# Cross attention on one Trainium2 core: query stacks in 6 transfers for 12, key parts written one by one, the sums read back later in the queue's order

## The chip, the cores and the metric

The kernel runs on one core of a Trainium2 chip. The metric is the device time of one execution in microseconds (us), the median of the timed runs. Five engines work side by side: TensorE (PE in the profile, with PEld for its weight loads), VectorE (DVE), ScalarE (ACT), GpSimd (POOL) and SyncE (SP). SP computes nothing here; it issues nearly all transfers between device memory (DRAM) and on-chip memory (SBUF), one after another, in the order in which they are written, and waits on semaphores between them.

## The reference

Four layers in a row on `x` of shape (32, 100, 128), with a context `ctx` of (32, 1444, 128) and a condition of (32, 128). Layers 0, 1 and 3 are transformer layers: modulated layer norm, self attention, cross attention to the context, feed forward. Layer 2 is a router with three experts. The change lies in the cross attention of the three transformer layers (here layer 3's; 16 heads of 8 channels, 100 queries, 1444 keys, 32 batches):

```python
xn = _ln(x)
q = _heads(xn @ q_w + q_b)
kv = (context @ kv_w + kv_b).reshape(B, S, 2, H, HD)
k = kv[:, :, 0].transpose(0, 2, 1, 3)
v = kv[:, :, 1].transpose(0, 2, 1, 3)
x_ca = _attend(q, k, v) @ ca_proj_w + ca_proj_b     # softmax(q k^T * SCALE) v, float32
x = x + x_ca
```

## The kernel before

All is float32, but scores go through bf16 matmuls: a float32 query or key is split into three bf16 parts (high, middle, low), and six of the nine products of parts are added up inside one matmul, whose contracted rows hold 8 channels times 6 slots (48 rows, `CROWS`), for the 8 heads of one half `e` of the array at rows 64·e and up. `SLOT_Q` and `SLOT_K` say which part stands in which slot. So each batch needs a query stack `qst` (48 rows for each half, 8 heads × 100 tokens along a row) and a key stack `kst` (128 rows × 8 heads × 1444 keys) in SBUF. Both come from DRAM: the query parts lie in `g.qx` from an earlier phase, and the key stack is put together in DRAM (`g.kscr`), because one key part goes to several slots.

`cross_attention_phase` is called for layers 0, 1 and 3 with `context` "normed", "raw" and "kept"; these words name the three phases below. It works as a pipeline over 32 batches, one slot for each batch; three buffers (`LAG`) of every kind turn. In slot b:

- PE makes the transposed context, keys and values of batches b+3 and b+2 (`pe_prep`), score tiles of batches b+1 and b+2 for the row maxima only (`pe_max`, line 1169, 48 tiles a batch, read by DVE at line 1349), then the transposed scores of batch b (`pe_scores`, line 1192), of which ACT takes exponentials (line 1296), and their products with the values (`pe_values`, line 1209). The order on PE is written out in `PLANS`.
- DVE turns the maxima of b+1 into three bf16 parts `nparts` (`dve_negmax`, the last step is line 1373). `pe_scores` of the next slot starts only when these lie in the query stack (`neg_loaded`).
- POOL splits the keys of b+3 into `parts` (`pool_split_keys`: for each cut of the columns copy, subtract, copy, subtract, lines 1401, 1428, 1401, 1432). One cut in the normed phase, three in the others. Before it overwrites `parts` it waits until the former batch's key transfers have landed (`k_written`).
- SP runs `sp_slot`, the queue order at issue here: `sp_stacks` (b+2; it waits for `k_written`, then loads `kst`, one transfer at line 1460, and `qst`, twelve at line 1467), `sp_load_ctx` (b+5), `sp_out` (b-1: the sums `osb` go to DRAM, line 1496; SP waits until they have landed; four transfers bring them back into `oT`, line 1500, and one the denominators into `den`), in the raw phase `sp_keep_ctx` (line 1481), `sp_negmax` (b+1, six at line 1476), `sp_keys_out` (b+3, six at line 1489).

The lines of that order are

```python
if slot.k(2) is not None:
    sp_stacks(slot.k(2))
if slot.k(5) is not None:
    sp_load_ctx(slot.k(5))
if slot.k(-1) is not None:
    sp_out(slot.k(-1))
...
if slot.k(1) is not None:
    sp_negmax(slot.k(1))
if slot.k(3) is not None:
    sp_keys_out(slot.k(3))
```

PE needs the stacks of b+2 about two thirds into slot b (tile 0 of `pe_max`), and the negative maxima of b+1 at the start of slot b+1.

Of the kernel before, what the change touches and what calls it, by code (L numbers as in the profile page):

```python
# [11 lines left out]
B = 32  # L12
N = 100
S = 1444
T = B * N
HEADS = 16
HD = P // HEADS
# [4 lines left out]
PAIRS = HEADS // 2  # L22
# [13 lines left out]


PARTS = 3
SLOT_K = (0, 1, 2, 0, 1, 0)
SLOT_Q = (0, 0, 0, 1, 1, 2)  # L40
HALF = 64
CROWS = HD * len(SLOT_K)
CROWS_NEG = CROWS + 3
# [7 lines left out]
def wait(eng, sem, value):  # L51

    if isinstance(value, int) and value <= 0:
        return
    eng.wait_ge(sem, value)
# [965 lines left out]
def cross_attention_phase(g, wk, kb, wv, context):  # L1021
# [15 lines left out]
    S1 = 6 if kept else 9  # L1037
    CUTS = [(0, S)] if normed else [(0, BANK), (BANK, 2 * BANK), (2 * BANK, S)]
    ST_BANK, O_BANK, RING = 0, 4 * BANK, 5 * BANK
    K_RUNS = ((0, 3), (3, 2), (5, 1))  # L1040
    KW = 16 * 2 * len(K_RUNS)
    Q_SLOTS = ((0, 3), (3, 2), (5, 1))

    plan = PLANS[context]
    PREP_INDEX = ({"K0": 0, "K1": 1, "K2": 2, "V0": 3, "V1": 4, "V2": 5} if kept else
# [7 lines left out]
    with ExitStack() as st:  # L1053
# [15 lines left out]
        parts = sb("kparts", [P, 3, S], BF16)  # L1069
# [9 lines left out]
        split, parts_ready = sem("split_steps"), sem("parts_ready")  # L1079
        k_written, k_loaded = slots("k_written"), slots("k_loaded")  # L1080
        qst_loaded, neg_loaded = slots("qstack_loaded"), slots("negmax_loaded")
# [9 lines left out]
        def slot_rows(s, e, first, n):  # L1091

            return g.kscr[s].rearrange("(e r d) (j n) -> e (d j) r n", e=2, d=HD, j=PAIRS)[e, :, first:first + n]

        def max_tile(slot, x):

            return (slot.k(1), x + MAX_A) if x < MT - MAX_A else (slot.k(2), x - (MT - MAX_A))
# [5 lines left out]
        def pe_ring_free(slot, tile):  # L1103

            for t, back in older[tile]:
                if t == "turn":
                    k = slot.k(1 + back)
                    if k is not None:
                        wait(g.pe, neg_steps, 4 * (k.b + 1))
                        return  # L1110
                elif isinstance(t, str):
                    k = slot.k((2 if t[0] == "V" else 3) + back)
                    if k is not None:
                        wait(g.pe, p_read, S1 * k.b + PREP_INDEX[t] + 1)
                        return
                else:
                    k = slot.k((1 if t < MT - MAX_A else 2) + back)
                    if k is not None:
                        wait(g.pe, m_read, MT * k.b + (t + MAX_A) % MT + 1)
                        return  # L1120
# [35 lines left out]
        def pe_max(slot, x):  # L1156

            k, t = max_tile(slot, x)
            if k is None:
                return  # L1160
            s, r = k.s, k.r
            if t == 0:
                wait(g.pe, k_loaded[s], 16 * (r + 1))
                wait(g.pe, qst_loaded[s], 16 * 12 * (r + 1))
            pe_ring_free(slot, x)
            at = bank_of(x)
            e, c, j = t % 2, (t // 2) % 3, t // 6
            a, w, row0 = starts[c], widths[c], HALF * e
            nc.tensor.matmul(ps[0:N, at:at + w], g.qst[s][row0:row0 + CROWS, j, :], g.kst[s][row0:row0 + CROWS, j, a:a + w],  # L1169
                             start=True, stop=True).then_inc(m_full, 1)  # L1170
# [246 lines left out]
        def pool_split_keys(k):  # L1417
# [3 lines left out]
            p = k.prev()  # L1421
            wait(pool, k_written[p.s], KW * (p.r + 1))
            for i, (a, z) in enumerate(CUTS):
# [18 lines left out]
        def sp_load_ctx(k):  # L1442
            b, s, r = k.b, k.s, k.r
            sp = g.sp
            if kept:
                wait(sp, p_full, S1 * (b - LAG + 1))
                sp.dma_start(turned[s][:, :], g.ctxT[b]).then_inc(ctx_loaded[s], 16)
                return
            wait(sp, p_full, S1 * (b - LAG) + 3)
            full = KT - 1  # L1450
            sp.dma_start(ctok[s][:, 0:full, :], g.ctx[bass.ds(b, 1), 0:128 * full, :].rearrange("a (k p) c -> p (a k) c", p=P)).then_inc(ctx_loaded[s], 16)
            sp.dma_start(ctok[s][0:kts[-1], full, :], g.ctx[bass.ds(b, 1), 128 * full:S, :].rearrange("a p c -> p (a c)")).then_inc(ctx_loaded[s], 16)

        def sp_stacks(k):

            b, s, r = k.b, k.s, k.r
            sp = g.sp
            wait(sp, st_full, H2 * (b - LAG + 1))
            wait(sp, k_written[s], KW * (r + 1))
            sp.dma_start(g.kst[s][:, :, :].rearrange("p j n -> p (j n)"), g.kscr[s]).then_inc(k_loaded[s], 16)  # L1460
            per = CH // N
            for e in range(2):
                for part, (first, copies) in enumerate(Q_SLOTS):
                    src = g.qx[b // per, e, part].rearrange("(d j) n -> d j n", j=PAIRS)[:, :, N * (b % per):N * (b % per) + N]
                    for slot in range(first, first + copies):
                        at = HALF * e + HD * slot
                        sp.dma_start(g.qst[s][at:at + HD, :, :], src).then_inc(qst_loaded[s], 16)

        def sp_negmax(k):
            b, s, r = k.b, k.s, k.r  # L1470
# [7 lines left out]
        def sp_keep_ctx(k):  # L1478
            b, s, sp = k.b, k.s, g.sp
            wait(sp, p_read, S1 * b + PREP_INDEX["T2"] + 1)  # L1480
            sp.dma_start(g.ctxT[b], turned[s][:, :]).then_inc(ctx_kept, 16)

        def sp_keys_out(k):
            b, s, r = k.b, k.s, k.r
            sp = g.sp
            wait(sp, parts_ready, len(CUTS) * (b + 1))
            for first, n in K_RUNS:
                for e in range(2):
                    sp.dma_start(slot_rows(s, e, first, n), parts[HALF * e:HALF * e + HALF, 0:n, :]).then_inc(k_written[s], 16)

        def sp_out(k):

            b, s, r = k.b, k.s, k.r
            sp = g.sp
            wait(sp, o_read, b + 1)
            sp.dma_start(g.oscr[s], osb[s][:, :]).then_inc(o_moved[s], 16)
            wait(sp, o_moved[s], 96 * r + 16)
            src = g.oscr[s].rearrange("(c r) (a n) -> a c r n", r=32, n=N)
            for a in range(4):
                sp.dma_start(g.oT[32 * a:32 * a + 32, bass.ds(b * N, N)], src[a, :, 0:HD, :]).then_inc(o_moved[s], 16)  # L1500
            per = CH // N
            sp.dma_start(g.den[b // per:P:NCH, N * (b % per):N * (b % per) + N], src[:, :, HD, :]).then_inc(o_moved[s], 16)

        def sp_slot(slot):
            if slot.k(2) is not None:
                sp_stacks(slot.k(2))
            if slot.k(5) is not None:
                sp_load_ctx(slot.k(5))
            if slot.k(-1) is not None:
                sp_out(slot.k(-1))  # L1510
            if context == "raw" and slot.k(3) is not None:
                sp_keep_ctx(slot.k(3))
            if slot.k(1) is not None:
# [3 lines that stand above are left out]
# [3 lines left out]
        known = lambda b: Slot(0, b, LAG, False)  # L1520
        looped = lambda i, u: Slot(i, u, LAG, True)
        first = known(0).k(0)

        with nc.Block() as block:
# [69 lines left out]
            @block.sync  # L1594
            def _(sp):
                g.sp = sp
                for b in range(LAG - 1):
                    sp_load_ctx(known(b).k(0))
                if normed:
                    sp.wait_ge(stacks_set, 1)  # L1600
                    for s in range(LAG):
                        for e in range(2):
                            rows = slice(HALF * e + CROWS, HALF * e + HALF)
                            sp.dma_start(g.kscr[s][rows, :], g.kst[0][rows, :, :].rearrange("p j n -> p (j n)")).then_inc(ones_written, 16)
                    sp.wait_ge(ones_written, 16 * 2 * LAG)
                for b in range(-3, 1):
                    sp_slot(known(b))
                for i in range(loops):
                    for u in range(1, LAG + 1):
                        sp_slot(looped(i, u))  # L1610
                for b in range(LAG * loops + 1, B):
                    sp_slot(known(b))
                sp_out(known(B - 1).k(0))
                if context == "raw":
                    sp.wait_ge(ctx_kept, 16 * B)
                for s in range(LAG):
                    sp.wait_ge(o_moved[s], 96 * len(range(s, B, LAG)))
# [573 lines left out]
```

## Time and profile before

| | |
|---|---|
| median of 3 runs | 5570.83 us (5566.85 to 5578.4) |
| the profiled execution | 5582.41 us, span of its instructions 5580.6 us |
| mean granted clock of TensorE | 0.864 of full speed |
| cross attention "normed" (layer 0) | from about 425 to 1712 us |
| cross attention "raw" (layer 1) | from about 2140 to 3354 us |
| cross attention "kept" (layer 3) | from about 4310 to 5472 us |
| busy share of the span | PE 86%, DVE 70%, ACT 53%, POOL 26% |

The table is read so: the profiled execution is one run of its own, 11.6 us above the median of the timed ones; a change in us that is worked out from its rows is subtracted from the median. The shares are means over phases with different limits, so they say little on a single phase; the three cross attentions together take some 3660 us, two thirds of the span, and what limits each is read from its own stretch.

### The profile page before, as it was taken

The numbers are of one execution on the slowest core, as the hardware profiler recorded it, in microseconds if no ns is written. First come the engines' busy times: TensorE is split into PE (matmuls) and PEld (weight loads), VectorE is DVE, ScalarE is ACT, GpSimd is POOL, SyncE is SP. The second block draws the span as 40 slices with busy tenths as digits, with TensorE's granted clock in tenths as the row PEclk, the third lists the DMA queues.
The fourth block names the chain that finished last, engine by engine and source line by source line (L and its number), as shares of the span: only waits on it lengthen the run. The fifth ranks groups of instructions, "written<-read, shape, count | busy, mean of one in ns | idle before, by whom it ended". The sixth has DMA issues, their size and how long they took to land. (4 is left out here: it accounts for less than half of the span.)

```text
span 5580.6 us, 168125 instructions
## 1 busy us (share of the span) xinstructions
PE 4790.3 (86%) x72434; PEld 3025.4 (54%) x72434; DVE 3913.3 (70%) x7814; ACT 2961.3 (53%) x4527; POOL 1466.4 (26%) x1189
## 2 busy tenths in 40 slices
PE   4858999999998585999999997888676799999998
PEld 2634555555554362666666663564364366656654
DVE  5547888888883553888888873465454688889893
ACT  2323666766655332666666663215423366666665
POOL 1013444434420103333333310000200334333320
PEclk6667999999988666999999988999766699999998
DMA  3325555555530334666666630550242565556640
GB/s 81 69 62 174 158 166 172 156 180 159 165 125 10 77 61 140 198 205 206 204 200 201 193 118 18 166 175 1 53 71 54 173 188 188 185 186 193 190 155 17
DMA packets 481664, 766.00 MB, mean 137 GB/s; under 512 B 144922, under 2 KB 381882, under 8 KB 468538
## 3 DMA queue, kind: packets, MB, share of 16 engines
q1 hardware_dynamic: 462394, 741.14, 44.5%
q10 hardware_dynamic: 18528, 14.11, 1.1%
q8 instruction: 571, 9.36, 0.7%
q14 instruction: 171, 1.40, 0.1%
HBM read 465.48 MB, written 287.75 MB: 135 GB/s over the span
## 5 line engine op out<-in xcount | busy, mean ns | idle before, releaser
L1349 DVE TENSOR_REDUCE maxima<-ps 100x1 f32<-100x482 f32 (+1 forms) x4608 | 2743.0, 650 | 580.3 <-PE ps L1169 566.5
L1296 ACT ACTIVATE probs<-ps 128x800 f32<-128x800 f32 (+1 forms) x2304 | 1805.6, 833 | 573.6 <-PE ps L1192 562.7
L1169 PE MATMUL ps<-kst,qst 48*100 48x482 bf16 (+1 forms) x4608 | 1392.6, 420 | 137.1 <-DMA qst<-cross_q_parts 54.9
L1401 POOL TENSOR_TENSOR kparts<-kf,zero 128x512 bf16<-128x512 f32 (+2 forms) x448 | 545.0, 1217 | 2044.2 <-ACT kf L1268 2004.1
L1209 PE MATMUL ps<-probs,vals 128*9 128x100 f32 x36864 | 1047.9, 256 | 1.0 <-ACT probs L1296 0.9
L1209 PEld LDWEIGHTS ps<-probs,vals 128*9 128x9 f32 x36864 | 757.5, 92 | 240.3 <-issue 198.8
L1169 PEld LDWEIGHTS ps<-kst,qst 48*100 48x100 bf16 x4608 | 443.8, 123 | 797.7 <-DVE maxima L1349 452.5
L1192 PE MATMUL ps<-qst,kst 51*128 51x100 bf16 x18432 | 803.8, 210 | 81.2 <-ACT probs L1296 60.6
L1192 PEld LDWEIGHTS ps<-qst,kst 51*128 51x128 bf16 x18432 | 614.4, 99 | 224.9 <-issue 86.4
L763 ACT ACTIVATE probs<-ps 100x800 f32<-100x800 f32 x192 | 159.7, 837 | 369.0 <-PE ps L711 368.6
L1146 PE MATMUL ps<-ctxT,perm_wk_L 128*128 128x512 f32 (+1 forms) x576 | 327.6, 656 | 31.9 <-DMA ctxT<-ctx_turned 17.1
L1268 ACT ACTIVATE kf<-ps,perm_b_L 128x512 f32<-128x512 f32 (+1 forms) x288 | 190.4, 662 | 271.9 <-PE ps L1146 255.8
L1274 ACT ACTIVATE vals<-ps 128x512 f32<-128x512 f32 (+1 forms) x288 | 162.1, 563 | 317.2 <-PE ps L1152 312.0
L1432 POOL TENSOR_TENSOR kparts<-kf,kparts 128x512 bf16<-128x512 f32 (+2 forms) x224 | 305.0, 1361 | 17.6
L1428 POOL TENSOR_TENSOR kf<-kf,kparts 128x512 f32<-128x512 f32 (+2 forms) x224 | 304.7, 1360 | 17.6
L775 DVE TENSOR_REDUCE maxima<-ps 100x4 f32<-100x400 f32 x384 | 205.6, 570 | 143.6 <-PE ps L689 142.8
L1152 PE MATMUL ps<-wkv_L,ctxT 128*128 128x128 f32 (+1 forms) x1536 | 262.7, 318 | 7.2 <-DVE maxima L1349 4.9
L689 PE MATMUL ps<-kst 96*100 96x100 bf16 x1152 | 142.7, 286 | 131.7 <-DMA kst<-k_parts 103.3
L1152 PEld LDWEIGHTS ps<-wkv_L,ctxT 128*128 128x128 f32 (+1 forms) x1536 | 211.1, 211 | 66.8 <-DVE maxima L1349 44.6
L1262 ACT ACTIVATE ctxT<-ps 128x512 f32<-128x512 f32 (+1 forms) x192 | 109.8, 572 | 178.8 <-PE ps L1138 178.8
L689 PEld LDWEIGHTS ps<-kst 96*100 96x100 bf16 x1152 | 118.0, 191 | 157.1 <-issue 105.1
L1138 PE MATMUL ps<-ident,ctok 128*128 128x128 f32 (+1 forms) x768 | 135.8, 295 | 63.7 <-POOL ctok L1414 43.4
(260 smaller groups left out, 4528.0 us busy)
## 6 DMA issues: line engine op xcount, KB each, us to landing
kst<-ctx_k_stack SPq DMA_DIRECT2D x96, 2888.0 KB
ctx_k_stack<-kparts SPq DMA_DIRECT2D x192, 541.5 KB
ctx_k_stack<-kparts SPq DMA_DIRECT2D x192, 361.0 KB
ctok<-in_ctx_dram SPq DMA_DIRECT2D x64, 704.0 KB
ctx_k_stack<-kparts SPq DMA_DIRECT2D x192, 180.5 KB
ctx_turned<-ctxT SPq DMA_DIRECT2D x32, 722.0 KB, 3.4
cT<-ctx_turned SPq DMA_DIRECT2D x32, 722.0 KB, 5.5
ctxT<-ctx_turned SPq DMA_DIRECT2D x32, 722.0 KB
```

What stands on the lines that cost most here:

```text
L689: ins = nc.tensor.matmul(ps[0:N, o:o + N], queries[s][0:SROWS, h // 2, q0:q0 + N], keys[0:SROWS, h // 2, k0:k0 + N], start=True, stop=True)
L775: nc.vector.tensor_reduce(maxima[:, t // 4, c:c + 4], ps[0:N, at:at + CH].rearrange("p (h k) -> p h k", h=4), AX.X, ALU.max).then_inc(m_re ...
L1146: ins = nc.tensor.matmul(ps[:, at:at + w], wk, turned[s][:, a:a + w], start=True, stop=True)
L1152: ins = nc.tensor.matmul(ps[0:n, at + 128 * q:at + 128 * q + 128], turned[s][:, 128 * kt:128 * kt + n], wv, start=True, stop=True)
L1169: nc.tensor.matmul(ps[0:N, at:at + w], g.qst[s][row0:row0 + CROWS, j, :], g.kst[s][row0:row0 + CROWS, j, a:a + w], start=True, stop=True). ...
L1192: ins = nc.tensor.matmul(ps[0:kts[kt], o:o + N], g.kst[s][rows, 4 * hf + jj, 128 * kt:128 * kt + kts[kt]], g.qst[s][rows, 4 * hf + jj, :], ...
L1209: ins = nc.tensor.matmul(ps[q:q + VW, o:o + N], vals[s][:, kt, h, :], probs[kt % 2][hf][:, N * (4 * e + jj):N * (4 * e + jj) + N], start=( ...
L1296: nc.scalar.activation(probs[kt % 2][hf][0:kts[kt], :].rearrange("p (k n) -> p k n", k=2), src, ACT.Exp).then_inc(exp_done, 1)
L1349: nc.vector.reduce_max(maxima[:, col:col + 1], ps[0:N, at:at + widths[c]], AX.X).then_inc(m_read, 1)
L1401: return nc.gpsimd.tensor_tensor(out, src, g.zero[0:src.shape[0], 0:1].to_broadcast(list(src.shape)), ALU.add)
L1428: nc.gpsimd.tensor_tensor(kf[:, a:z], kf[:, a:z], parts[:, 0, a:z], ALU.subtract).then_inc(split, 1)
L1432: nc.gpsimd.tensor_tensor(parts[:, 2, a:z], kf[:, a:z], parts[:, 1, a:z], ALU.subtract).then_inc(parts_ready, 1)
```

## The change

Three edits in `cross_attention_phase`. (1) The two tables of slots change places, so that the query slots hold parts 0, 1, 2, then 0, 1, then 0; the same six products are added up in another order. A run of slots now holds consecutive query parts, which lie one after the other in DRAM, so one transfer fills a run: 3 for each half, 6 for 12, with 24, 16 and 8 rows. (2) A run of key slots now holds copies of one part: part 0 goes to three slots, part 1 to two, part 2 to one. The six key transfers keep their sizes and places in DRAM, read one part repeatedly (`to_broadcast`) and each pair waits for its own part only: part 0 and 1 for steps 1 and 3 of POOL's last cut. (3) `sp_out` is cut in two: the sums go out before `sp_load_ctx` is issued, and are read back (`sp_out_back`) after it.

```diff
-SLOT_K = (0, 1, 2, 0, 1, 0)
-SLOT_Q = (0, 0, 0, 1, 1, 2)
+SLOT_K = (0, 0, 0, 1, 1, 2)
+SLOT_Q = (0, 1, 2, 0, 1, 0)
...
             for e in range(2):
-                for part, (first, copies) in enumerate(Q_SLOTS):
-                    src = g.qx[b // per, e, part].rearrange("(d j) n -> d j n", j=PAIRS)[:, :, N * (b % per):N * (b % per) + N]
-                    for slot in range(first, first + copies):
-                        at = HALF * e + HD * slot
-                        sp.dma_start(g.qst[s][at:at + HD, :, :], src).then_inc(qst_loaded[s], 16)
+                rows = g.qx[b // per, e].rearrange("t (d j) n -> (t d) j n", j=PAIRS)
+                for first, n in RUNS:
+                    at = HALF * e + HD * first
+                    sp.dma_start(g.qst[s][at:at + HD * n, :, :],
+                                 rows[0:HD * n, :, N * (b % per):N * (b % per) + N]).then_inc(qst_loaded[s], 16)
...
         def sp_keys_out(k):
             b, s, r = k.b, k.s, k.r
             sp = g.sp
-            wait(sp, parts_ready, len(CUTS) * (b + 1))
-            for first, n in K_RUNS:
+            for part, (first, n) in enumerate(RUNS):
+                if part < 2:
+                    wait(sp, split, 3 * (len(CUTS) * (b + 1) - 1) + (1, 3)[part])
+                else:
+                    wait(sp, parts_ready, len(CUTS) * (b + 1))
                 for e in range(2):
-                    sp.dma_start(slot_rows(s, e, first, n), parts[HALF * e:HALF * e + HALF, 0:n, :]).then_inc(k_written[s], 16)
+                    sp.dma_start(slot_rows(s, e, first, n),
+                                 parts[HALF * e:HALF * e + HALF, part:part + 1, :].to_broadcast([HALF, n, S])).then_inc(k_written[s], 16)
...
             sp.dma_start(g.oscr[s], osb[s][:, :]).then_inc(o_moved[s], 16)
+
+        def sp_out_back(k):
...
             wait(sp, o_moved[s], 96 * r + 16)
...
+            if slot.k(-1) is not None:
+                sp_out(slot.k(-1))
             if slot.k(5) is not None:
                 sp_load_ctx(slot.k(5))
             if slot.k(-1) is not None:
-                sp_out(slot.k(-1))
+                sp_out_back(slot.k(-1))
```

On SP, in a slot of the kept phase, these rows stood from one key stack's load to the read back of the sums (`kst`, `qst` the stacks, `ctxT` the context, `o_sums` the sums in DRAM):

```order
L1460 DMA kst_417<-ctx_k_stack 128x11552
L1467 DMA qst_417<-cross_q_parts 8x8x100 x12
L1447 DMA ctxT_507<-ctx_turned 128x1444
L1496 DMA o_sums<-osb_507 128x400
L1500 DMA oT<-o_sums 32x1x100 x4
L1502 DMA den<-o_sums 16x1x100
L1476 DMA qst_417<-nparts 1x8x100 x6
```

The same place after the change:

```order
L1459 DMA kst_417<-ctx_k_stack 128x11552
L1465 DMA qst_417<-cross_q_parts 24x8x100
L1465 DMA qst_417<-cross_q_parts 16x8x100
L1465 DMA qst_417<-cross_q_parts 8x8x100
L1465 DMA qst_417<-cross_q_parts 24x8x100
L1465 DMA qst_417<-cross_q_parts 16x8x100
L1465 DMA qst_417<-cross_q_parts 8x8x100
L1499 DMA o_sums<-osb_507 128x400
L1446 DMA ctxT_507<-ctx_turned 128x1444
L1508 DMA oT<-o_sums 32x1x100 x4
L1510 DMA den<-o_sums 16x1x100
L1475 DMA qst_417<-nparts 1x8x100 x6
```

Six transfers stand where twelve stood, and the write of the sums has moved ahead of the context's load, its read back has stayed behind it.

The key transfers of the same slot, before, with their waits (`modulated_29` is the number that `parts_ready` has here):

```order
L1476 DMA qst_417<-nparts 1x8x100 x5
L1489 DMA ctx_k_stack<-kparts 64x3x1444 [waits modulated_29]
L1489 DMA ctx_k_stack<-kparts 64x3x1444
L1489 DMA ctx_k_stack<-kparts 64x2x1444 x2
L1489 DMA ctx_k_stack<-kparts 64x1444 x2
```

and after (`scaled_28` is the number of `split`, the count of POOL's steps):

```order
L1475 DMA qst_417<-nparts 1x8x100 x5
L1491 DMA ctx_k_stack<-kparts 64x3x1444 [waits scaled_28]
L1491 DMA ctx_k_stack<-kparts 64x3x1444
L1491 DMA ctx_k_stack<-kparts 64x2x1444 [waits scaled_28]
L1491 DMA ctx_k_stack<-kparts 64x2x1444
L1491 DMA ctx_k_stack<-kparts 64x1444 [waits modulated_29]
L1491 DMA ctx_k_stack<-kparts 64x1444
```

The six transfers have kept their shapes and their place in the queue; one wait became three, of which only the last is for the end of POOL's split.

## Rows read from the trace of the kernel before

**Rows 1.** One line's instructions, raw phase, steady stretch: the row maxima, one a batch.

```profile
L1355 DVE TENSOR_REDUCE rowmax<-maxima x29: 202/203/204, 2263.8 to 3252.9; 100x16 f32<-100x48 f32 x29
```

**Rows 2.** The same, kept phase, steady stretch.

```profile
L1355 DVE TENSOR_REDUCE rowmax<-maxima x29: 202/203/204, 4435.9 to 5381.1; 100x16 f32<-100x48 f32 x29
```

**Rows 3.** Windows: us, busy us (instructions) of each engine, granted clock, DMA share, GB/s.

```profile
2555.90:2589.90 34.00, 33.75 (x677) 21.57 (x670) 30.00 (x55) 24.15 (x35) 12.46 (x12) 1.00 0.64 204
...
2802.10:2841.10 39.00, 38.91 (x668) 25.30 (x670) 29.06 (x53) 24.10 (x34) 12.45 (x12) 0.84 0.62 192
4650.90:4682.90 32.00, 31.35 (x660) 20.25 (x656) 29.71 (x55) 22.30 (x32) 12.47 (x12) 1.00 0.62 197
```

**Rows 4.** Waits of PE, raw, 2308 to 3263 us: total us, times, longest.

```profile
PE ps L1192 <- DMA qst<-nparts: 17.2, 14, 2.5
```

**Rows 5.** Waits of PE, kept, 4478 to 5391 us.

```profile
PE ps L1169 <- DMA kst<-ctx_k_stack: 6.6, 4, 2.0
```

**Rows 6.** Waits of SP, raw, 2308 to 3263 us.

```profile
SPq L1476 <- DVE nparts L1373: 9.1, 5, 2.3
```

**Rows 7.** Waits of SP, kept, 4430 to 5390 us.

```profile
SPq L1500 <- DMA o_sums<-osb: 115.3, 28, 5.5
...
SPq L1476 <- DVE nparts L1373: 9.8, 2, 9.2
```

**Rows 8.** Waits of SP, normed, 530 to 1580 us.

```profile
SPq L1476 <- DVE nparts L1373: 76.6, 27, 6.8
SPq L1489 <- POOL kparts L1432: 53.2, 27, 2.0
```

**Rows 9.** Timeline of SP, one kept slot: start us, us, line, transfer.

```profile
4725.74 0.33 SPq L1460 DMA_DIRECT2D kst<-ctx_k_stack  x1
4726.11 8.34 SPq L1467 DMA_DIRECT2D qst<-cross_q_parts  x12
...
4734.98 0.43 SPq L1496 DMA_DIRECT2D o_sums<-osb  x1
4739.74 2.55 SPq L1500 DMA_DIRECT2D oT<-o_sums  x4
...
4747.45 9.29 SPq L1489 DMA_DIRECT2D ctx_k_stack<-kparts  x6
4759.26 0.33 SPq L1460 DMA_DIRECT2D kst<-ctx_k_stack  x1
```

**Rows 10.** Transfers from 4725 to 4745 us: GB/s in 40 slices of 0.5 us.

```profile
GB/s 6 0 0 647 92 0 462 277 554 323 554 370 370 554 277 601 310 462 79 110 116 268 174 277 393 396 349 130 13 33 0 0 26 18 12 21 58 13 3 0
...
ctxT<-ctx_turned SPq DMA_DIRECT2D x1, 722.0 KB
```

**Rows 11.** Timeline of SP, end of the kept phase: the last sums.

```profile
5471.34 0.32 SPq L1496 DMA_DIRECT2D o_sums<-osb  x1
5473.23 2.54 SPq L1500 DMA_DIRECT2D oT<-o_sums  x4
```

**Rows 12.** Single lines: ns of one issue on SP, min/median/max, first and last start.

```profile
L1467 SPq DMA_DIRECT2D qst<-cross_q_parts x1152: 632/646/1328, 426.3 to 5407.4; - x192
```

**Rows 13.** The same, the negative maxima.

```profile
L1476 SPq DMA_DIRECT2D qst<-nparts x576: 634/635/1588, 484.9 to 5448.5; - x192
```

**Rows 14.** The same, the context's load.

```profile
L1451 SPq DMA_DIRECT2D ctok<-in_ctx_dram x64: 384/448/1087, 381.1 to 3178.6; - x64
```

**Rows 15.** Timeline of PE, start of the raw phase: the first maximum tile.

```profile
2187.27 0.64 PE L1169 MATMUL ps<-kst,qst 48*100 48x482 bf16 x2 [25.62 <-DMA qst<-cross_q_parts]
```

**Rows 16.** Timeline of POOL, start of the raw phase: the last cut of the first split.

```profile
2160.59 0.89 POOL L1401 TENSOR_TENSOR kparts<-kf,zero 128x420 bf16<-128x420 f32 x1
...
2163.57 0.98 POOL L1432 TENSOR_TENSOR kparts<-kf,kparts 128x420 bf16<-128x420 f32 x1
```

**Rows 17.** Timeline of SP, start of the raw phase.

```profile
2164.57 8.59 SPq L1489 DMA_DIRECT2D ctx_k_stack<-kparts  x6
2175.38 0.36 SPq L1460 DMA_DIRECT2D kst<-ctx_k_stack  x1
```

More of the change, by code:

```diff
@@ L1039, in cross_attention_phase @@
     ST_BANK, O_BANK, RING = 0, 4 * BANK, 5 * BANK
-    K_RUNS = ((0, 3), (3, 2), (5, 1))
-    KW = 16 * 2 * len(K_RUNS)
-    Q_SLOTS = ((0, 3), (3, 2), (5, 1))
+    RUNS = ((0, 3), (3, 2), (5, 1))
+    KW = 16 * 2 * len(RUNS)
     plan = PLANS[context]
@@ L1163, in pe_max @@
                 wait(g.pe, k_loaded[s], 16 * (r + 1))
-                wait(g.pe, qst_loaded[s], 16 * 12 * (r + 1))
+                wait(g.pe, qst_loaded[s], 16 * 2 * len(RUNS) * (r + 1))
             pe_ring_free(slot, x)
@@ L1496, in sp_out @@
             sp.dma_start(g.oscr[s], osb[s][:, :]).then_inc(o_moved[s], 16)
+        def sp_out_back(k):
+            b, s, r = k.b, k.s, k.r
+            sp = g.sp
             wait(sp, o_moved[s], 96 * r + 16)
@@ L1613, in _ @@
                 sp_out(known(B - 1).k(0))
+                sp_out_back(known(B - 1).k(0))
                 if context == "raw":
```

## The prediction, made before the changed kernel had run

> **What bounds the kernel now.** I read the stage windows first and took the three cross attentions apart, because two thirds of the span lie there and the diff touches nothing else. Then I took for each phase the time per batch, SP's waits, PE's waits, and single slots.
>
> Time per batch is read from an instruction that runs once a batch. In the raw phase 28 intervals take 3252.9 − 2263.8 = 989.1 us, 35.33 us each [rows 1]; in the kept phase 5381.1 − 4435.9 = 945.2 us, 33.76 each [rows 2].
>
> Is that PE's pace? Three slots answer, each cut from the first score matmul to the next one [rows 3]. One raw slot takes 34.0 us with PE busy for 33.75 of them, one kept slot 32.0 with 31.35. These are what PE's own work takes when nothing holds it: the floors. A third slot with the same work takes 39.0 us, at a mean granted clock of 0.84 for 1.00, so part of it ran at 1.2 for 2.4 GHz. It begins at 2802.1, right after a wait of PE for the negative maxima; PE had such waits in 14 of the raw slots [rows 4], and in the kept phase waits for the key stack [rows 5]. So short waits for transfers, and the low clock after them, make up the 1.3 and 1.8 us between mean and floor.
>
> Why are the transfers late? SP's waits tell. In the normed phase SP waits for DVE's maxima in each of 27 slots, 76.6 us, and for POOL, 53.2 us [rows 8]: it is early by 4.8 us a slot, and engines set the pace. In the raw phase the first of these waits has shrunk to 9.1 us in 27 slots [rows 6], in the kept phase to 9.8 in 28, nearly all of it in one [rows 7]. There SP goes round without waiting for any engine; what it still waits for is transfers of its own, such as 115.3 us in 28 slots for the sums to land, 4.1 us a slot [rows 7]. One kept turn shows it [rows 9]: from 4725.74 to 4759.26, 33.52 us, issues and landings end to end. **In raw and kept the queue on SP sets the pace**, by 1.3 and 1.8 us a slot over PE.
>
> **The change part by part.**
>
> *Sums ahead of the context's load.* In that turn the sums are issued at 4734.98 and have landed by 4739.74, after 4.76 us; the last ones of the phase, with an empty queue, land in 1.89 us (5471.34 to 5473.23) [rows 11]. What stands before them is read from the slices [rows 10]: the key stack runs from about 4726.5 to 4734, a slow stretch with the query rows to about 4736.5, then 722 KB of context and the sums at some 390 GB/s until 4739. So transfers are served about in the order of issue, and the sums, 200 KB, came last. Without the context ahead of them they land 722 × 1024 B / 390 GB/s = 1.9 us earlier, say 2.0 with the 0.44 us issue. That is the lower bound. The upper adds half of the slow stretch of 2.5 us, if six query transfers need half the time of twelve: 3.3 us. I take the middle, 2.6.
>
> *Six query transfers for twelve.* Issue of one takes 0.646 us [rows 12], so up to 6 × 0.65 = 3.9 us less. But this doesn't add to the 2.6: the sums behind still wait for the key stack ahead of them, which runs to about 8.3 us after its issue. Issued earlier, they only wait longer. The saving is covered by that stack; if the cover were gone it would be 3.9. The price of a 24-row transfer is in no row. Eight short runs cost 0.635 us [rows 13], 64 cost 0.646 [rows 12], a load of 1408 runs (11 × 128 in its shape) 0.448 [rows 14]: no growth with the count, so I take 0.65; the other end is three times that, 1.94 for 24 rows, and no saving at all.
>
> The Trainium skill speaks against this edit: in Perfetto Trace Analysis, section What "DMA-bound" means, the issuing engine's track is time of descriptor generation, and large descriptors are what helps. Here the runs stay 200 B and their number stays the same, so by that rule the twelve times 0.65 us would remain. The three rows above disagree with it as far as they go; what it gives is the second case below.
>
> *Key parts one by one.* In the steady slots the sizes and the order stay, and SP arrives after POOL has finished in raw and kept, so nothing is gained but room. In the normed phase the start moves up 2 us a slot, which is slack. It counts at the start of a phase: in the raw one POOL's first step of the last cut ends at 2161.48, the last at 2164.55 [rows 16], and the keys go at 2164.57 [rows 17]. The first pair can go 3.1 us earlier. The first maximum tile follows the key stack's issue by 11.9 us (2175.38 [rows 17] to 2187.27 [rows 15]), waiting for the query rows; with half as many I take 1 us off (0 to 1.8). PE had been idle for 25.62 us, so all 4 us come off the phase. The other two starts have the same steps; 3 × 4 = 12 us.
>
> *The new turn of the queue.* Kept: 33.76 − 2.6 = 31.2 us (30.5 to 31.8), raw at least the same off: 35.33 − 2.6 = 32.7. Both are under the floors of 32.0 and 34.0, by 0.8 and 1.3 us, so SP begins to wait for DVE's maxima as in the normed phase, PE no longer waits, and the low clock after its waits goes. What is late next is PE itself. In kept the margin is small, so I put 32.2 for 32.0. Gains: raw (35.33 − 34.0) × 28 = 37 us, kept (33.76 − 32.2) × 28 = 44 us. The first and last three slots of a phase I leave as they are. Normed: no steady gain.
>
> **Sum:** 37 + 44 + 12 = 93 us. The profiled execution took 5582.41 us (span 5580.6 and 1.8 around it), which gives 5489; it lies 11.6 above the median of the timed runs, 5570.83, from which I forecast **5478 us**, 1.7% less. A difference under 0.2% (11 us) could not be told from none.
>
> **The rivals.**
>
> *The queue still sets the pace* (the query issues keep their time, or the sums gain only the 2.0). Then the turns are 31.8 and 33.3 before any unevenness, at the floors, and some slots still end in a wait and a low clock. For it: the spread of issue times, 632 to 1328 ns for one transfer [rows 12]; against: it needs both edits to do their least. Half the gain, 22 + 19, and 9 at the starts: 50 us, 5521.
>
> *The floors are not floors.* The short slots may be short because the wait before them let DVE, ACT and POOL run ahead, and then PE would be held by them. For it: single slots can't show what a long row of them takes. Against: DVE is busy for 30.0 of 34.0 us and 29.7 of 32.0, ACT for 24.2 and 22.3 [rows 3]. Then only the starts remain: 5559, a change at the edge of what can be told.
>
> *Slower: the repeated source.* Each key transfer now reads one SBUF row two or three times. From issue to landing the keys take 4747.45 to 4759.26, 11.8 us [rows 9]. If copies of one row are drawn one behind the other, this phase grows; from 2.6 us of growth (22%) the turn is as long as before, and beyond it the kernel is slower. At half as long again, +5.9 us: kept 31.2 + 5.9 = 37.1, raw 38.6, against 33.76 and 35.33, so (3.3 + 3.3) × 28 = 185 less the 12 of the starts: 5744. Against it: before, the three parts of a row came from the same partitions too, and the shapes of the transfers have not changed. The Trainium skill has a harder form of it: DMA: Bandwidth & Descriptors, Rules for kernel authors, says that a leading broadcast of c copies confines a transfer to at most c of the 16 engines. In the order's rows the leading count is still 64, not the copies, so the rule should not bite, and no run here shows such a case; that keeps this rival at its small chance.
>
> **How the numbers follow.** 0.62 for the forecast (its own range 5460 to 5500: floors met in full and the runs' spread of 6 us below, a kept slot of 32.8 above), 0.25 for the queue that still sets the pace, 0.08 for the false floors, 0.04 for slower, 0.01 for a gain beyond the floors. The range of 8 in 10 takes the forecast and most of the second case: 5450 to 5530. Faster by over 0.2%: 0.62 + 0.25 + 0.01 + a little of the third, 0.89; within: 0.07; slower: 0.04.
>
> **What would show it.** Time per batch of 34.0 and 32.2 us in raw and kept, no other in normed; SP waiting for DVE's maxima in nearly every slot of raw and kept; PE's waits for the maxima and the key stack gone, granted clock near 1.00 in the steady stretches; sums landed some 11.4 us after the key stack's issue (14.0 before); query issues of 0.65 us each whatever their rows; six key transfers in about 9 us as before; first maximum tiles 4 us earlier. Wrong if SP is early and time per batch stays (false floors), if query issues take 1.3 to 1.9 us, or if the keys take over 14 us from issue to landing.

## The result and the profile after

The changed kernel takes 5491.75 us (median of 4 runs, 5476.65 to 5503.66), the kernel before on the same chip 5574.61: a ratio of 0.9849 with a 95% interval of 0.9818 to 0.9879, 83 us less (67 to 101). Timed again beside other kernels (below) the ratio was 0.9838 (0.9816 to 0.9860), 90 us less. The profiled execution took 5503.66 us, span 5501.9.

Time per batch first: the row maxima in the steady stretch of raw, then of kept, as in [rows 1, 2].

```profile
L1354 DVE TENSOR_REDUCE rowmax<-maxima x29: 202/203/204, 2263.0 to 3214.6; 100x16 f32<-100x48 f32 x29
...
L1354 DVE TENSOR_REDUCE rowmax<-maxima x29: 202/203/203, 4394.5 to 5297.6; 100x16 f32<-100x48 f32 x29
```

Raw: 951.6 / 28 = 33.99 us for 35.33. Kept: 903.1 / 28 = 32.25 for 33.76. That is 37.5 + 42.1 = 80 us. The windows from a phase's first score matmul to its last batch's show what PE did in them (columns as in [rows 3]). First the kernel before, raw and kept:

```profile
2237.00:3263.00 1026.00, 1002.05 (x19316) 638.63 (x19313) 868.58 (x1567) 699.08 (x986) 361.08 (x348) 0.97 0.64 201
4411.00:5391.00 980.00, 930.94 (x18966) 599.45 (x18964) 864.51 (x1566) 646.67 (x899) 362.39 (x348) 0.97 0.60 189
```

and the changed one:

```profile
2237.00:3226.00 989.00, 979.53 (x19339) 625.38 (x19341) 866.57 (x1567) 699.90 (x988) 361.68 (x348) 1.00 0.67 209
4370.00:5308.00 938.00, 911.95 (x18973) 589.91 (x18968) 862.01 (x1567) 646.39 (x900) 362.72 (x348) 0.99 0.63 197
```

Same work, but PE is busy 22.5 and 19 us less for it, at a granted clock of 1.00 and 0.99 for 0.97, and idle less (9.5 for 24 us in raw, 26 for 49 in kept). DVE, ACT and POOL have not changed.

SP's waits in raw, then kept, then normed (530 to 1580 us), to be laid beside [rows 6 to 8]:

```profile
SPq L1475 <- DVE nparts L1372: 66.1, 29, 10.3
SPq L1508 <- DMA o_sums<-osb: 54.2, 28, 5.3
...
SPq L1508 <- DMA o_sums<-osb: 144.7, 28, 5.8
...
SPq L1475 <- DVE nparts L1372: 34.9, 19, 13.4
...
SPq L1475 <- DVE nparts L1372: 207.6, 27, 9.8
```

In raw SP now waits for DVE's maxima in every slot, in kept in 19: the queue has become early. Leaving out one wait of 10.3 and 13.4 us at a phase's start, it is 2.0 us a slot in raw and 0.8 in kept. PE's waits in raw no longer name a transfer; in kept three small ones are left (first raw, then kept):

```profile
PE ps L1168 <- DVE maxima L1348: 4.5, 28, 0.2
PE ps L1208 <- issue: 2.1, 5, 0.7
...
PE ps L1168 <- DMA kst<-ctx_k_stack: 3.5, 3, 1.4
PE ps L1168 <- issue: 3.0, 4, 1.4
```

Before, kept had more such waits than the four of [rows 5]. Thirteen more at the same line (4478 to 5391 us) have no releaser that the profile shows:

```profile
PE ps L1169 <- issue: 20.7, 13, 3.0
```

Those over 0.5 us end 12.0 to 13.4 us after a key stack's issue, where the first tile of a phase comes too (11.9 us), so they are taken here as waits for the stacks; of 17 with 27.3 us in all, 7 with 6.5 are left.

One kept turn of SP (once round its list, for one slot), beside the turn of [rows 9]:

```profile
4671.86 0.34 SPq L1459 DMA_DIRECT2D kst<-ctx_k_stack  x1
4672.24 4.85 SPq L1465 DMA_DIRECT2D qst<-cross_q_parts  x6
4677.14 1.71 SPq L1499 DMA_DIRECT2D o_sums<-osb  x1
4678.89 0.43 SPq L1446 DMA_DIRECT2D ctxT<-ctx_turned  x1
4684.38 2.55 SPq L1508 DMA_DIRECT2D oT<-o_sums  x4
...
4688.68 4.13 SPq L1475 DMA_DIRECT2D qst<-nparts  x6
4692.85 8.88 SPq L1491 DMA_DIRECT2D ctx_k_stack<-kparts  x6
4703.95 0.33 SPq L1459 DMA_DIRECT2D kst<-ctx_k_stack  x1
```

The query issues take 4.85 us for 8.34. The sums go out 5.3 us after the key stack for 9.2, but are read back 12.5 us after it for 14.0: of the 3.9 us won at the issue, 1.5 are left at the landing here. As a mean of 23 slots the read back comes 12.2 us after the key stack's issue in raw (15.2 before) and 12.3 in kept (14.5 before).

The start of the raw phase (SP, POOL's last step of the first split, the first maximum tile on PE):

```profile
2163.77 8.59 SPq L1491 DMA_DIRECT2D ctx_k_stack<-kparts  x6
2174.59 0.36 SPq L1459 DMA_DIRECT2D kst<-ctx_k_stack  x1
...
2165.84 0.98 POOL L1431 TENSOR_TENSOR kparts<-kf,kparts 128x420 bf16<-128x420 f32 x1
...
2186.25 0.64 PE L1168 MATMUL ps<-kst,qst 48*100 48x482 bf16 x2 [22.03 <-DMA qst<-cross_q_parts]
```

Against POOL's end (2166.82) the keys go 3.05 us earlier, and the first tile follows after 19.4 us for 22.7 in [rows 15, 16]: 3.3 us. The same difference is 3.0 us in normed and 4.2 in kept.

### The profile page after: what moved, and what is told of

Same layout as the page of the kernel before. It is cut to its first block and busy times, and to the rows that moved or that the text cites. A ratio compares the mean times of both kernels' runs of the same rounds, so it can differ in the third digit from the quotient of the medians.

```text
span 5501.9 us, 167549 instructions
## 1 busy us (share of the span) xinstructions
PE 4762.0 (87%) x72434; PEld 3010.4 (55%) x72434; DVE 3909.5 (71%) x7814; ACT 2963.6 (54%) x4527; POOL 1467.9 (27%) x1189
```

## The experiments

The question is which edit brought the 83 us, and through what. **Theory:** in raw and kept a slot takes PE's own time or SP's turn, whichever is longer; the sums, no longer waiting behind the context, brought the turn below PE's time. **Rival:** the 4 us of query issue that a slot saves are what counts. The ratios are to the kernel before, timed on the same chip.

**Each edit alone.** *Edit 3 alone*, twelve query transfers and one wait for the keys kept:

```diff
...
+            if slot.k(-1) is not None:
+                sp_out(slot.k(-1))
             if slot.k(5) is not None:
                 sp_load_ctx(slot.k(5))
             if slot.k(-1) is not None:
-                sp_out(slot.k(-1))
+                sp_out_back(slot.k(-1))
```

What moves is the sums' write; their read back keeps its place in the queue's order, behind the context's load.

> The kernel before with edit 3 alone: the sums' write goes ahead of the context's load; twelve query transfers, keys after one wait. Theory (the order of the sums does it): the sums are read back 12.3 to 12.6 us after the key stack's issue for 15 before, raw and kept fall to 34.0 to 34.2 and 32.3 to 32.6 us a batch, 65 to 75 us less than the kernel before. Rival (the query issues, 4 us a slot, do it): about a quarter to a half of the 83 us, 20 to 40 us less, with time per batch near 34.7 and 33.1.

0.9851 (0.9839 to 0.9864), 83 us less: as much as the whole change, and more than the 65 to 75 us expected. The sums are read back 12.8 (raw) and 12.5 us (kept) after the key stack's issue, 2.4 and 2.0 earlier than before (means of 23 slots). Per batch 33.87 and 32.30:

```profile
L1355 DVE TENSOR_REDUCE rowmax<-maxima x29: 202/203/204, 2264.9 to 3213.2; 100x16 f32<-100x48 f32 x29
...
L1355 DVE TENSOR_REDUCE rowmax<-maxima x29: 202/203/204, 4388.1 to 5292.4; 100x16 f32<-100x48 f32 x29
```

*Edit 1 alone* (six query transfers, the sums behind the context as before; as the two tables change places, the key transfers read one part repeatedly here too, after one wait for all):

```diff
...
-                wait(g.pe, qst_loaded[s], 16 * 12 * (r + 1))
+                wait(g.pe, qst_loaded[s], 16 * 2 * len(RUNS) * (r + 1))
...
+                rows = g.qx[b // per, e].rearrange("t (d j) n -> (t d) j n", j=PAIRS)
+                for first, n in RUNS:
...
```

> The kernel before with edit 1 alone: six query transfers for twelve, in the old order of the queue, keys after one wait for all. Theory: the 4 us of issue are freed, but the sums still wait behind key stack and context, and are read back 14.0 to 14.8 us after the key stack's issue (15 before); 0 to 25 us less. Rival (the query issues do it): read back near 12.5 us, 45 to 75 us less.

0.9968 (0.9956 to 0.9980), 18 us less. Where the rest of the saved issue time went stands, for kept, in SP's waits (4403 to 5379 us), beside the row for the sums in [rows 7]:

```profile
SPq L1500 <- DMA o_sums<-osb: 197.7, 28, 8.0
```

SP waits for the sums 82 us longer than before, 2.9 us a slot. The queries' issue takes 4.4 us a slot for 8.0 (means of 23 slots): of the 3.6 us saved, 2.9 became waiting for the same landing, and another 1.0 went into a longer issue of the context's load (1.47 us for 0.49).

In raw the saving went another way. SP waits for the sums as long as before (110.2 us in 27 slots from 2308 to 3263 us, 110.7 before), but the issue of the context's second load has grown (2237 to 3263 us; first the kernel before):

```profile
L1452 SPq DMA_DIRECT2D ctok<-in_ctx_dram x27: 496/810/2010, 2254.9 to 3179.1; - x27
...
L1451 SPq DMA_DIRECT2D ctok<-in_ctx_dram x27: 3170/4117/5400, 2255.4 to 3171.9; - x27
```

The queries take 4.47 us a slot for 7.98, the context's two loads 5.42 for 1.46 (means of 23 slots): nothing is freed ahead of the sums.

*Edit 2 alone* (keys part by part, with the tables changed and one part read repeatedly; twelve query transfers, old order):

```diff
...
-            wait(sp, parts_ready, len(CUTS) * (b + 1))
-            for first, n in K_RUNS:
+            for part, (first, n) in enumerate(RUNS):
+                if part < 2:
+                    wait(sp, split, 3 * (len(CUTS) * (b + 1) - 1) + (1, 3)[part])
+                else:
+                    wait(sp, parts_ready, len(CUTS) * (b + 1))
...
```

> The kernel before with edit 2 alone: key parts written one by one as they are made, from a source row read two or three times; twelve query transfers, old order of the queue. Theory: only the three starts of a phase are shorter, by some 3 us each, 9 us less in all (5 to 12), time per batch as before. Rival (waiting for the split paces the steady slots too): 20 us less or more. If the repeated source cost anything, keys from issue to landing over 12.5 us and a kernel that is slower.

0.9981 (0.9970 to 0.9992), 11 us less; per batch 35.23 and 33.63, the first tiles of normed, raw and kept 2.1, 3.1 and 3.7 us earlier against POOL's end. It is the starts, as the theory has it, and no cost of the repeated source shows: at the start of raw it is 10.9 us from the first key transfer's issue to the key stack's, for 10.8 before.

*Edits 1 and 2, without 3* (against the changed kernel):

```diff
-            if slot.k(-1) is not None:
-                sp_out(slot.k(-1))
             if slot.k(5) is not None:
                 sp_load_ctx(slot.k(5))
             if slot.k(-1) is not None:
-                sp_out_back(slot.k(-1))
+                sp_out(slot.k(-1))
```

> The changed kernel without edit 3: six query transfers and key parts one by one, but the sums' write behind the context's load as before. Theory: 10 to 35 us less than the kernel before, raw and kept at 34.9 to 35.3 and 33.2 to 33.7 us a batch. Rival (the query issues do it): 55 to 83 us less, time per batch like the changed kernel's 33.99 and 32.25.

0.9953 (0.9940 to 0.9966), 26 us less, per batch 34.73 (a little under the 34.9 to 35.3 expected) and 33.38. The rival's 55 us or more are excluded.

**What is left for the others once the sums go first.** The changed kernel again, and edits 2 and 3 with twelve query transfers:

```diff
-                rows = g.qx[b // per, e].rearrange("t (d j) n -> (t d) j n", j=PAIRS)
-                for first, n in RUNS:
...
+                for slot, part in enumerate(SLOT_Q):
...
```

> The changed kernel itself, timed beside the next three, since edit 3 alone gave 81.5 us of the 84. If the other two edits add nothing once the sums go ahead: 80 to 85 us less than before. If they add what they gave in the old order (24 us): 105 us less, which the interval of the first comparison (0.9818 to 0.9879) just excludes.

> The changed kernel with twelve query transfers of 8 rows, so edits 2 and 3 alone. Theory (with the sums ahead, SP has room in every slot and issue time is free): the same time as the changed kernel within 5 us. Rival (4 us of issue a slot still count): 15 us or more above it.

0.9838 (0.9816 to 0.9860) and 0.9836 (0.9815 to 0.9858): with the sums ahead, six transfers for twelve are worth nothing that can be told.

**Is it PE's own time that ends the gain?** The read back of the sums is moved behind the keys:

```diff
-            if slot.k(-1) is not None:
-                sp_out_back(slot.k(-1))
             if context == "raw" and slot.k(3) is not None:
                 sp_keep_ctx(slot.k(3))
             if slot.k(1) is not None:
                 sp_negmax(slot.k(1))
             if slot.k(3) is not None:
                 sp_keys_out(slot.k(3))
+            if slot.k(-1) is not None:
+                sp_out_back(slot.k(-1))
```

> The changed kernel with the read back of the sums put behind the key transfers, into the time in which SP waits for the keys to land; the wait for the sums (5.8 us a slot in kept) goes. Theory (PE's own work is the floor, 32.0 and 33.85 to 34.0): kept goes from 32.25 to 32.0, raw stays at 33.9, 3 to 10 us less than the changed kernel and no more. Rival (SP's turn is still what is felt): 28 x 2 us or more in raw and kept, over 50 us less.

0.9833 (0.9810 to 0.9857), not to be told from the changed kernel. Kept, a waits row of SP (4400 to 5290 us) and of its batches:

```profile
SPq L1475 <- DVE nparts L1372: 237.8, 28, 9.1
```

```profile
L1354 DVE TENSOR_REDUCE rowmax<-maxima x29: 202/203/204, 4384.3 to 5281.3; 100x16 f32<-100x48 f32 x29
```

SP now has 8.5 us to spare in every slot, and a batch takes 897.0 / 28 = 32.04 us. That is the floor of [rows 3], and it is real: beyond it SP's time buys nothing. Raw, where SP has 6.6 us to spare, takes 34.04.

**Queries and sums ahead of the key stack:**

```diff
+            if slot.k(2) is not None and (slot.looped or slot.b != -2):
+                sp_queries(slot.k(2))
+            if slot.k(-1) is not None:
+                sp_out(slot.k(-1))
             if slot.k(2) is not None:
                 sp_stacks(slot.k(2))
-            if slot.k(-1) is not None:
-                sp_out(slot.k(-1))
...
+            if not slot.looped and slot.b == -3:
+                sp_queries(slot.k(3))
             if slot.k(3) is not None:
                 sp_keys_out(slot.k(3))
```

> The changed kernel with the query rows and the sums' write issued ahead of the key stack, before SP waits for the keys to land (at a phase's start ahead of the first key transfers), so that neither waits behind 2.9 MB. Theory: the first maximum tile of a phase follows the key stack's issue by 8.3 us, not 11.5, 9 us off the three starts, and kept at 32.0: 10 to 17 us less than the changed kernel. Rival (the tile waits for the key stack's landing, not for the query rows): no change at the starts, 0 to 7 us less. A risk: six issues of 0.8 us ahead of the key stack make it later by 2 us a slot.

0.9874 (0.9854 to 0.9894), 14 us above the changed kernel timed beside it, by the medians: the theory's number was wrong, the risk named came true. SP and PE in kept (4366 to 5320 us):

```profile
SPq L1480 <- DVE nparts L1372: 275.8, 29, 13.5
```

```profile
PE ps L1168 <- DMA kst<-ctx_k_stack: 17.1, 19, 2.1
```

SP has over 9 us to spare a slot, and yet PE waits for the key stack in 19 slots, and a batch takes 918.5 / 28 = 32.80 us:

```profile
L1354 DVE TENSOR_REDUCE rowmax<-maxima x29: 202/203/204, 4392.7 to 5311.2; 100x16 f32<-100x48 f32 x29
```

The timeline shows why:

```profile
4721.05 4.79 SPq L1480 DMA_DIRECT2D qst<-nparts  x6
4725.89 8.78 SPq L1496 DMA_DIRECT2D ctx_k_stack<-kparts  x6
4734.71 4.36 SPq L1463 DMA_DIRECT2D qst<-cross_q_parts  x6
...
4739.60 0.43 SPq L1471 DMA_DIRECT2D kst<-ctx_k_stack  x1
```

From the maxima, whose time DVE sets, to the key stack's issue it takes 18.6 us, for 15.3 in the changed kernel. So there is a second limit beside the turn: the chain from the maxima over the keys to the stack. At the starts of raw and kept the first tile came another 1.6 and 1.1 us earlier, not 3: the tile still follows the key stack's issue by 10.1 and 10.2 us, so the stack itself needs most of the 11.5 us. In normed it came 3.5 us later, since SP was still issuing queries when the keys were ready.

**Is it what stands ahead of the sums?** In the kept phase each context is loaded twice, the second time into a buffer that nobody reads; once in the kernel before, where it stands ahead of the sums, once in edit 3 alone, where it stands behind them. The same line in both (PE also waits for both loads of a batch):

```diff
...
                 sp.dma_start(turned[s][:, :], g.ctxT[b]).then_inc(ctx_loaded[s], 16)
+                sp.dma_start(spare[s][:, :], g.ctxT[b]).then_inc(ctx_loaded[s], 16)
```

> The kernel before, with the context of each batch loaded twice in the kept phase (a second load of 722 KB into a spare buffer right behind the first), so twice as much stands ahead of the sums in the queue. Theory (the sums wait for what was issued ahead of them, and SP's turn paces the phase): the sums are read back 1.9 us later, kept goes from 33.76 to 35.5 us a batch or more, 45 to 60 us more than the kernel before; raw and normed as they were. Rival (the sums' place in the queue is not what counts): under 15 us more.

> The same second load in the kernel with edit 3 alone, where the context stands behind the sums' write. Theory: the same bytes are moved but nothing waits behind them, kept stays at 32.0 to 32.4 us a batch, ratio to the kernel before 0.985 as without the load. Rival (the bytes themselves cost, by traffic beside the other transfers): kept grows by as much as it does with the load ahead of the sums.

Ahead: 1.0095 (1.0076 to 1.0114), 53 us more. Behind: 0.9847 (0.9824 to 0.9870), as without the load. The kept batches of the first, 1002.5 / 28 = 35.80 us, and a slot:

```profile
L1356 DVE TENSOR_REDUCE rowmax<-maxima x29: 202/203/204, 4442.4 to 5444.9; 100x16 f32<-100x48 f32 x29
```

```profile
4714.90 0.33 SPq L1462 DMA_DIRECT2D kst<-ctx_k_stack  x1
...
4725.23 0.43 SPq L1498 DMA_DIRECT2D o_sums<-osb  x1
4730.85 2.55 SPq L1502 DMA_DIRECT2D oT<-o_sums  x4
```

and of the second, 900.8 / 28 = 32.17:

```profile
L1356 DVE TENSOR_REDUCE rowmax<-maxima x29: 202/203/204, 4396.6 to 5297.4; 100x16 f32<-100x48 f32 x29
```

The sums are read back 16.0 us after the key stack (14.0 in [rows 9]; means 16.8 and 14.5), 2.0 us later here and 2.3 as a mean, and the batch grows by 2.0 us. The bytes themselves cost nothing that shows. This pair shows the theory best: 722 KB are worth 2 us a slot where something waits behind them, and nothing behind the sums.

**The context behind the read back**, and then behind the maxima too:

```diff
-            if slot.k(5) is not None:
-                sp_load_ctx(slot.k(5))
             if slot.k(-1) is not None:
                 sp_out(slot.k(-1))
+            if slot.k(5) is not None:
+                sp_load_ctx(slot.k(5))
```

> The kernel before with the context's load put behind the read back of the sums, so that the sums wait neither for it nor does it use their landing time. Theory: the sums are read back 12.5 us after the key stack's issue as with edit 3 alone, 60 to 85 us less than the kernel before. Rival (the gain of edit 3 is that the context is loaded while SP waits for the sums): under 25 us less.

0.9914 (0.9890 to 0.9938), 48 us less: between the two, so neither number came. The sums are read back 12.7 us after the key stack, as expected, and kept comes to 32.49 us; but raw stays at 982.5 / 28 = 35.09, with 13 waits of PE (2240 to 3260 us; 14 before, [rows 4]) for the maxima, which now stand behind the context:

```profile
L1355 DVE TENSOR_REDUCE rowmax<-maxima x29: 202/203/204, 2268.1 to 3250.6; 100x16 f32<-100x48 f32 x29
...
PE ps L1192 <- DMA qst<-nparts: 12.8, 13, 2.3
```

The second step, against the first:

```diff
+            if slot.k(1) is not None:
+                sp_negmax(slot.k(1))
             if slot.k(5) is not None:
                 sp_load_ctx(slot.k(5))
             if context == "raw" and slot.k(3) is not None:
                 sp_keep_ctx(slot.k(3))
-            if slot.k(1) is not None:
-                sp_negmax(slot.k(1))
```

> The kernel before with the context's load (and in raw the write of its turned copy) put behind the negative maxima as well, so that neither the sums nor the maxima stand behind it. It asks why raw stayed at 35.1 us a batch with the context right behind the sums. If the maxima's landing behind the context's bytes held PE there: raw comes to 34.0 to 34.3, PE's waits for the maxima go, some 75 us less than the kernel before. If it is SP's turn, which now holds the context's three issues (1.5 to 2 us) outside the sums' landing time: raw stays at 34.9 to 35.2, about 48 us less.

0.9942 (0.9919 to 0.9965), 32 us less, neither the 75 of the first case nor the 48 of the second. PE's waits for the maxima are gone, yet raw takes 973.5 / 28 = 34.77 us, just under the 34.9 to 35.2 of the second case, and kept 32.74. In PE's waits of raw (2290 to 3180 us) others stand in their place, ahead of the maximum tiles:

```profile
L1355 DVE TENSOR_REDUCE rowmax<-maxima x29: 202/203/204, 2259.2 to 3232.7; 100x16 f32<-100x48 f32 x29
...
PE ps L1169 <- issue: 15.0, 15, 2.6
```

The first tile of a batch follows the key stack's issue by 12.7 us (mean of 23 slots; 15.0 with edit 3 alone), close to the 12.0 at the phase's start where it waits for the stacks, and SP waits for DVE's maxima in only 2 of these slots. So raw is held by SP's turn, and the wait only moves from the maxima to the stacks. The turn carries the context's issues outside the sums' landing time, which the expectation named; what it did not name is that the six key issues, now right behind the context, take 9.8 us a slot for 8.6 with edit 3 alone. The order of edit 3 does both: the sums go early, and the context's issue lies in the time in which SP waits for them anyway.

## Why the prediction was right

| its term | predicted | measured |
|---|---|---|
| raw, per batch | 34.0, 37 us in all | 33.99, 37.5 us |
| kept, per batch | 32.2, 44 us | 32.25 and 32.05, 42 and 48 us |
| three starts | 12 us | 3.0 + 3.3 + 4.2 = 10.5 us |
| sums read back after the key stack's issue | 11.4 us | 12.2 and 12.3 |
| SP's turn, raw and kept | 32.7 and 31.2 | about 32.0 and 31.5 (batch less SP's wait for DVE) |
| in all | 93 us | 83 and 90 us |

*The queue paces raw and kept.* Right: in kept the doubled context brought the sums 2.3 us later and the batch grew by 2.0, and in raw edit 3 alone brought them 2.4 us earlier and the batch fell from 35.33 to 33.87. Normed had room and did not move (38.80 before, 38.92 and 38.83 after).

*The sums ahead of the context.* This was the step that carried the forecast, and alone it gave all of the steady gain. The size of 2.6 us was near: 2.2 in kept, 3.0 in raw as means. With edit 3 alone it was 2.0 in kept, the lower bound, and that was enough. (1.9 and 0.44 us make 2.3, not the 2.0 of the prediction; the sizes measured run from 2.0 to 3.0.) The 11.4 us after the key stack came from one slot with 14.0; the means before were 15.2 and 14.5.

*Six transfers for twelve.* One takes 0.68 us as a median, 0.81 as a mean of the slot shown, near the 0.65 that I took and far from 1.94:

```profile
L1465 SPq DMA_DIRECT2D qst<-cross_q_parts x576: 582/680/2157, 423.1 to 5319.7; - x192
```

That the edit adds nothing to the sums' step was forecast, and with the sums ahead it added nothing that can be told. The reason given, that the key stack covers the saving, was right in kept: with edit 1 alone 2.9 us of the 3.6 saved came back as waiting. In raw the step was another: the saving came back as issue time of what follows. In the changed kernel the queries take 4.36 us a slot there for 7.98, but the context's loads 3.95 for 1.46 and the sums' write 1.47 for 0.48, 9.8 us in all for 9.9 (means of 23 slots). The second load in raw (2237 to 3226 us), beside the two rows of edit 1 alone:

```profile
L1451 SPq DMA_DIRECT2D ctok<-in_ctx_dram x27: 2108/3122/5021, 2251.6 to 3138.9; - x27
```

By the rule of the Trainium skill (Perfetto Trace Analysis, What "DMA-bound" means) the issue time would have stayed, as large descriptors are what helps. For the queries' own issues the trace differs, 4.85 us for 8.34 in the slot shown with runs of the same 200 B, and so it does for the three together in kept (6.4 us for 9.2); in raw, where the three take 9.8 us for 9.9, it agrees.

*The starts.* Of the 4 us each, the 3.1 of the keys came, in normed 2.6. The 1 us for the query rows was too much: 0.2 to 0.6. The key stack itself takes most of that time, as the kernel with the queries ahead showed.

*The rivals.* "The queue still sets the pace" was close in kept, where SP's wait for DVE is 0.8 us a slot. Its price of half the gain was wrong, though: edit 3 alone is its case, nothing from the query issues and 2.0 us (kept) from the sums, and the gain was whole. "The floors are not floors" fell: 32.04 over 28 slots with SP idle. "Slower by the repeated source" fell: key issues of 8.88 us for 9.29 and 2.2 us from their end to the next key stack's issue for 2.5.

The forecast of 5478 lies 14 us under the median: 10 in the gain (83 for 93) and 4 because the kernel before ran at 5574.61 beside it, not 5570.83. The terms read from the traces come to 90 us; the 3 us by which the normed stretch was longer in the profiled run (1126.6 for 1123.4) and some 5 us at the ends of the phases went against them, and did not show in the second profile of the same kernel in that size (1124.1). Whether edits 1 and 2 add their 10 us of starts to edit 3 within a run stays open: the intervals of 0.9838, 0.9849 and 0.9851 overlap.

## What to carry to other kernels

Where one queue issues nearly everything, work out its turn and compare it with the busiest engine's time for the same slot: here each microsecond counted until the turn was below it, and none after that. Look for what a wait in the queue stands behind: a short write that the queue waits for belongs ahead of a large load that is needed late, and the load's issue then lies in the wait. Fewer issues ahead of a wait that ends with a landing lengthened the wait, or the issues in between, and bought little (18 us of 5581 alone); and a queue with time to spare can still be late if a chain through it grew.

## What the runs showed of the hardware

The same transfer took longer to issue where it came sooner behind the key stack's 2.9 MB: the sums' write, 5.2 us after that stack's issue instead of 9.5 (means of 23 slots), took a median of 1.420 us in kept for 0.622 (the second row is the changed kernel's). The context's second load in raw, above, took 4.117 us behind six query transfers for 0.810 behind twelve. In kept with edit 1 alone it was the context's load, the next in line, that took longer (1.47 us for 0.49), and not the write (0.54). Where the queries go ahead of the key stack and the context's two loads follow it at once (the kernel with queries and sums ahead), the loads take 7.1 us a slot in raw, for 1.46 behind twelve query transfers; so it is how soon they come after the stack that goes with the longer issue, and not the shape of the query transfers.

```profile
L1496 SPq DMA_DIRECT2D o_sums<-osb x28: 430/622/1615, 4463.9 to 5376.7; - x28
```

```profile
L1499 SPq DMA_DIRECT2D o_sums<-osb x28: 323/1420/2693, 4418.1 to 5289.4; - x28
```

And 722 KB more a slot (doubled context, behind the sums) cost nothing that could be told, in a phase in which the changed kernel's DMA share is 0.63 without them.
